# A new order of work inside a group of heads, for both attentions of a two-layer kernel

## The reference

```python
# layer 0: 16 heads of 16 columns; two softmaxes over the same values
scores = einsum('bhid,bhjd->bhij', q, k) / sqrt(hd)
std_out = out_proj(softmax(where(mask, scores, neg)))
gsa_scores = scores + position_sensitivity * splat_attn
gsa_out = out_proj(softmax(where(mask, gsa_scores, neg)))
return (1.0 - blend) * std_out + blend * gsa_out
# layer 1: 16 heads of 16 columns; one softmax, scaled scores, causal
probs = softmax(where(causal, einsum('bqhd,bkhd->bhqk', q, k) * scale, min))
out = einsum('bhqk,bkhd->bqhd', probs, v)
```

## Time and profile before

| | |
|---|---|
| runs of the kernel before | 2149.99 us median of 3 (2125.07 to 2183.54) |
| the profiled execution | 2145.68 us, of which the span is 2143.8 us |
| mean granted TensorE clock | 0.857 of full |
| first attention (16 groups) | about 206 to 748 us of the span |
| second attention (8 groups) | about 1688 to 1931 us of the span |
| PE, DVE, ACT busy over the span | 87%, 72%, 60% |

### The profile page before, as it was taken

One profiled execution on the slowest core, in us unless ns is written; L12 is line 12 of the kernel. 1 busy time (PEld: TensorE's weight loads), 2 busy tenths in 40 slices (PEclk: granted clock), 3 DMA queues, 4 the chain that ended last, 5 costly groups with the idle time before them and its releaser, 6 DMA issues. The chain is left out here.

```text
span 2143.8 us, 32204 instructions
## 1 busy us (share of the span) xinstructions
PE 1855.6 (87%) x10498; PEld 1261.3 (59%) x10498; DVE 1549.8 (72%) x3465; ACT 1289.5 (60%) x2904; POOL 587.3 (27%) x1144
## 2 busy tenths in 40 slices
PE   4988899999999888788888988887778699997998
PEld 3557444545445377666667776666656344436787
DVE  7655766878777266999997789999446678835554
ACT  2533456767667633799986679998523277775111
POOL 2002011122112203545553445455123011113400
PEclk9999566989878899888879998888979599988999
DMA  2453131332231010000000000000015423101000
GB/s 109 158 157 60 30 60 31 61 61 53 38 61 31 2 66 1 1 1 1 1 1 1 1 1 1 1 1 1 0 44 143 102 55 61 37 2 66 1 1 40
DMA packets 36133, 82.53 MB, mean 38 GB/s; under 512 B 9600, under 2 KB 11776, under 8 KB 34944
## 3 DMA queue, kind: packets, MB, share of 16 engines
q1 hardware_dynamic: 35968, 80.48, 15.4%
HBM read 52.79 MB, written 27.26 MB: 37 GB/s over the span
## 5 line engine op out<-in xcount | busy, mean ns | idle before, releaser
L1030 ACT ACTIVATE probs<-pss 128x512 f32<-128x512 f32 (+3 forms) x1152 | 489.2, 493 | 233.7 <-PE pss L993 228.3
L1058 DVE TENSOR_REDUCE negmax<-px 128x2 f32<-128x1024 f32 (+2 forms) x480 | 515.3, 1114 | 148.2 <-PE px L974 145.6
L993 PE MATMUL pss<-queries,keys 49*128 49x512 f32 (+3 forms) x1152 | 335.8, 437 | 19.0 <-ACT probs L1030 12.1
L974 PE MATMUL px<-keys,queries 48*128 48x512 f32 (+3 forms) x1152 | 298.5, 470 | 11.5 <-DVE negmax L1058 7.5
L1563 POOL TENSOR_SCALAR rp<-sw,tau 128x256 f32<-128x256 f32 x576 | 275.5, 507 | 63.7 <-DVE st L1709 56.6
L993 PEld LDWEIGHTS pss<-queries,keys 49*128 49x128 f32 x1152 | 191.8, 216 | 166.4 <-ACT probs L1030 114.0
L1007 PE MATMUL po<-probs,vals 128*32 128x512 f32 (+3 forms) x2304 | 278.8, 580 | 2.2 <-POOL probs L1106 1.2
L1391 PE MATMUL pt<-ident,sw 128*128 128x128 f32 x768 | 160.5, 350 | 114.0 <-ACT sw L1474 70.1
L1462 ACT ACTIVATE ra<-sw,neg 128x256 f32<-128x256 f32 x576 | 243.6, 519 | 1.6 <-DVE neg L1685 1.6
L1106 POOL TENSOR_SCALAR_AFFINE_SELECT probs<-probs 128x512 f32<-128x512 f32 x192 | 120.8, 637 | 429.4 <-ACT probs L1030 429.4
L1406 PE MATMUL pss<-again,sw 128*128 128x256 f32 x1024 | 236.5, 394 | 0.0
(11 more groups left out here) (352 smaller groups left out, 2610.7 us busy)
## 6 DMA issues: line engine op xcount, KB each, us to landing
queries<-rec_q SPq DMA_DIRECT2D x96, 128.0 KB, 3.5
keys<-rec_k SPq DMA_DIRECT2D x96, 128.0 KB, 3.7
queries<-rec_q SPq DMA_DIRECT2D x96, 64.0 KB, 3.5
keys<-rec_k SPq DMA_DIRECT2D x96, 64.0 KB, 3.5
rec_q<-fs SPq DMA_DIRECT2D x16, 256.0 KB, 4.5
rec_k<-fs SPq DMA_DIRECT2D x16, 256.0 KB, 4.8
rec_q<-vals SPq DMA_DIRECT2D x16, 256.0 KB
rec_k<-vals SPq DMA_DIRECT2D x16, 256.0 KB
```

Of the source, the lines that this page charges most:

```text
L974: x = e.matmul(px[:, n, s * width:(s + 1) * width], ops.qs[p][at:at + STACK, tile, t * P:(t + 1) * P], ops.ks[p][at:at + STACK, tile, c:c ...
L993: e.matmul(tl.pss[scores % 3][:, 512 - width:512], ops.ks[p][at:at + STACK + 1, tile, j * P:(j + 1) * P], ops.qs[p][at:at + STACK + 1, til ...
L1030: e.activation(tl.probs[arg][:, w, :], tl.pss[scores % 3][:, 512 - width:512], ACT.Exp).then_inc(self.exp_made, 1)
L1058: e.tensor_reduce(out, from_px, X_AXIS, ALU.max, negate=True).then_inc(self.x_read, 1)
```

## The change

Only the two strings of `ORDERS` are replaced. Every group has the same letters as before: 48 `s`, 20 `m`, 12 `v`, 2 `d`, 2 `t` and 1 `r`.

```diff
-    ORDERS = {1: "msmssmsvsmsmssvvdsmsmssssmsssmsmssvsmmssvsmssvmssdvsmsmvsssmvssmsmvsmssvsssvrtssstsss", 2: "mmsssmsmmsssvvmssmsssmsssmsdsmssvmsssmvmssvvdmssmsvsmssvssmstsstsmssmssvmsssvvrssvsss"}
+    ORDERS = {1: "mmsssvmssmsvmsssmvsmsssmsssdmssstsmssmvmsssmvsmsvvdssmsmvsssmvmsssmvssmsvsssrtsssvsss", 2: "mmssvmsmssvmssmsvsmsssmsmsssvsmdsssmvsmssmvsmssvsmsvsmssdmsmssvmsssmvsssvrsssttsssvss"}
```

## The result

| | before | after |
|---|---|---|
| median of the runs | 2140.17 us of 4 (2125.07 to 2183.54) | 2036.70 us of 4 (2032.55 to 2043.96) |
| ratio of the two | | 0.9552, 95% interval 0.9481 to 0.9623 |
| profiled execution (span) | 2145.68 (2143.8) | 2033.01 (2031.1) |
| mean granted clock | 0.857 | 0.903 |

The changed kernel is 4.5% faster. I had forecast 1.2% and a range that ended at 2080, so the forecast was wrong: right in sign, a quarter of the size. The ratio leaves out executions over 1.5% above the fastest of the same kernel, here the one of 2183.54. The changed kernel, run six times more beside two experiments, gave 2036.74 (2035.29 to 2046.06) against 2134.42 of 11, ratio 0.9541 (0.9500 to 0.9581).

The account below looks back on a forecast made before the run. The prediction held that DVE limits most of a full-clock group and the low clock costs extra: 2145.7 + 0 - 18 - 9 + 1 + 0 = 2119.7, stated as 2125 us for the median, range 2080 to 2165.

Parts of the forecast that it names:

- What bounds the kernel: First attention: low clock costs 3.1 us a group, 34.8 at the start; at full clock DVE limits most of a group.
- Turns to the row stretch: Layer 0: both turns moved behind the rows, DVE stretch -1.87 us, row stretch 4.4 to 5.0; 0 a group, bounds -0.7, +1.0.
- The text's own test: Layer 0: a full-clock group shorter than 26.6 us would refute the view that the turns only change places.
- Changes of kind: Layer 0: 23 to 27 switches between kinds of PE work a group; 0 under DVE's reductions, 8 us if uncovered.
- The clock: Layer 0, groups 3 to 14: spread sums halve the low clock's loss of 37.3, -18 us, bounds 0 and -37.
- The start: Layer 0, groups 0 to 2: a quarter of the 34.8 us lost is regained, -9, bounds 0 and -35.
- The end: End of layer 0's stage: four sums instead of two follow the last score, partly in PE's idle time; +1 us.
- Layer 1: Second attention: one turn goes from the row stretch into the DVE-bound one; 0 us, bounds -3 and +5.
- The holding clock: Rival, chance 0.25: no steady group falls and the start recovers most of its 34.8 us; 2089 us.
- The clock that stays: Rival, chance 0.20: falls move to the new thin places and cost as much; only order counts, about 2157 us.
- The lasting low clock: Rival, chance 0.10: evenly spaced sums may not lift a low clock, each such group costs 10 us; 2200 us.

## Why the prediction was wrong

**What bounds the kernel.** Right: the clock was worth 3.1 us a group and 34.8 at the start, DVE bound the group at full clock, and the falls came where PE had no sums though it was busy. The one fall left in the changed kernel shows the same. First all engines, then the sums alone, in the 3.4 us before it:

```profile
559.80:563.20 3.40, 3.01 (x26) 1.57 (x24) 3.40 (x4) 3.40 (x8) 0.00 (x0) 1.00 0.02 5
...
559.80:563.20 3.40, 0.55 (x12) 0.16 (x8) 1.00 0.02 5
```

It lies in the V3 to V4 way, as named. But I had looked at one long way of the order before only, V11p to V0. The one ahead of V10p was as long, 4.2 us, and five of the eleven falls began there; the new order cuts it with V8p and V9p.

**Turns to the row stretch: the mis-sized term.** I took 0 a group and got -1.4, outside my bound of -0.7. The row stretch was right: 4.4 to 5.0 forecast, 4.5 measured. The turns' 1.84 against 1.87 too. Wrong was that DVE's idle time in the other stretch would stay; I allowed half of 1.5 us as a bound, and 1.16 of 1.48 went. I had sized the sums only as work on PE, 0.99 alone against 0.87 beside another, and not asked what DVE has in hand when each comes. The largest piece of the idle time before, 0.66 of 1.48, stood ahead of m16, behind V5 and four scores:

```profile
426.92 1.23 DVE L1058 TENSOR_REDUCE negmax<-px 128x2 f32<-128x1024 f32 x1 [0.66 <-PE px L974]
```

The new order has no such load between two maxima, and the wait is gone. The neighbouring sums of before weren't what DVE waited for in this stretch: they are 256 and 128 wide, and DVE idled 0.18 us behind one pair and not at all behind the other. The idle time that went makes -1.16 x 16 = -19 us. The text's own test (a group under 26.6 means that the view is wrong) fired. One sum of this part was off, too: 4.4 to 5.0, less 2.90 and 1.87, is -0.4 to +0.2 a group, not 0.0 to +0.2.

**Changes of kind.** Four more a group were to cost nothing under DVE's reductions, 8 us uncovered. They cost nothing that shows. (23 to 27 counts the rows as a kind of their own. With sums and rows as one kind, as the text has it, it is 22 to 26, and 25 to 27 in layer 1.) The Trainium skill (TensorEngine Tiling (Array Packing), Key Properties) says that changing the tiling mode drains TensorE; the up to 8 us that I had put beside that rule were not seen in the end time.

**The clock.** Halving the loss of groups 3 to 14 was the second mis-sized term: -18 forecast, -36 measured. I counted the places in which a fall can begin, two of 1.4 us each, against a fall in nearly every group, and took the V3 to V4 way as 3.6 us long, by DVE's reductions. It measures 2.7 us. The way with 2.5 to 2.7 us free of sums had 5 falls in 84 groups over all runs, while one with 4.0 to 4.2 had 5 to 11 in 12. I also left the turns out: I treated only sums as what holds the clock, so I did not see that the turn moved in layer 1 cuts the long way there. With layer 1's turn put back the way was 5.1 us and 4 of 6 groups fell.

**The start.** -9 forecast, -33 measured (of the 34.8 lost, 2.0 are left), at the far bound. The clump of V7 to V9 is not needed to lift a low clock, and it doesn't do it soon: the evenly spread order lifts it within group 0, while the old order with moved turns keeps its clump and has low spells of 34 us. Why the spread order lifts it earlier was not tried.

**The end.** +1 forecast. From the last group's row maxima to the stage's last instruction it was 37.5 us before and 34.3 after, but with 17.1 and 6.8 us at the low clock, so the term can't be told from the clock.

**Layer 1.** 0 with bounds -3 and +5, and it was about -19. I read 0.99 as nothing to gain and missed that the turn's place sets the 27.0 us there as well: behind the rows it stood between DVE and m0, in the middle it lies among reductions.

**The rivals.** The holding clock (0.25) came true as to the clock, and with its 2089 it was nearest, but it lacked the shorter group and layer 1: 2089 - 22 - 19 = 2048. The clock that stays (0.20), for which the Trainium skill stood with its rule on busyness and idle gaps (TensorE: Matmul & The Clock Gate, Part 1), is not what happened: before and after PE is nearly always busy, and the falls went; two stretches with PE busy 2.53 and 2.51 us of 3.40 in one kernel ended differently, and with V11p later the clock fell behind 3.40 us of 3.40. There the measurement decides against busy time as the rule. The lasting low clock (0.10), 2200 us, did not come with this change, but came with half of it (2200.12 with the turns alone; that the number is the same is chance).

**The range.** It should have been wider on the side of the gain. I had bounds of -11, -37, -35 and -3 in the text, -86 in sum, which is 2064, and took 2080 for the low end, as if these were independent; they share one cause, the spread, and came together. The rest, to 2037, is the idle time of DVE beyond its bound and layer 1.

## What to carry to other kernels

When an order of work is changed in two ways, ask for each wait of the bounding engine what that engine has in hand when the long instruction comes, and price the parts together: here, in a group at full clock, the new sums alone cost 1.3 us, the turns alone by estimate 0.9, and both together gained 1.4. In the end time the turns alone were 2.9% slower, the new sums alone (with layer 1's new order) 1.5% faster, and all together 4.5%. When the clock falls on a busy PE, list PE's ways that lack the dense kinds of matmul (here sums and turns), and break the longest ones; one small sum in the wrong place made six low spells in twelve groups instead of one. It is no sure cure: one order had falls in a way of 2.0 us. Terms that share a cause belong at the same end of the range.

## What the runs showed of the hardware

- The granted clock fell from 2.4 to 1.2 GHz with PE busy 3.40, 3.35, 3.01 and 2.51 of 3.40 us, and stayed with 2.53. What these falls had in common was few or no sums and turns (0 to 0.55 us of sums), the matmuls over 128 rows, and much work of 48 and 49 rows. That it is the rows, and not something else of these matmuls, was not tried. fp32 transposes by the identity (turns) helped to hold the clock: taking two from a place made falls there in layer 0, and taking one away in layer 1 made 4 in 6 groups. One of them (0.63 us) with no sum beside it did not hold it.
- At 1.2 GHz the clock can stay low with PE busy all the time: groups of 40.5 us with 39.97 of PE work, in the order that has its sums in clumps.
- Several orders show the falls in a strict period over groups (every second group with the turns back; four groups of 26.1, 26.1, 27.6 and 32.8 with V11p early; three of 33.0, 28.6 and 30.5 in most of the kernel before), so one group alone says nothing of an order's clock: read a dozen.
- In two stretches above with five scores or more between two sums, PE waited 0.23 us for ACT, though ACT is busy only 20.7 of 26.8 us of such a group (the kernel with V4 earlier).
